# Sorted rows that carry their expert shares, and one VectorE reduction per gathered tile

## What is computed

```python
x = L0_attn_x                      # (8, 512, 256)
xn = _layernorm(x)
scores = sigmoid(xn @ gate_w)      # (tokens, 32)
topk_w, topk_i = top_k(scores, 6)
topk_w = topk_w / (sum(topk_w) + 1e-20)
combine = sum(one_hot(topk_i, 32) * topk_w[..., None], axis=1)
act = silu(xn @ wg[e]) * (xn @ wu[e])
routed = einsum('tef,efd,te->td', act, wd, combine)
x = x + attention(xn) + routed + shared(xn)
```

## Time and profile before

| | |
|---|---|
| median of 3 runs | 1434.82 us (1430.83 to 1435.81) |
| the profiled execution | 1436.87 us, its span 1434.7 us |
| PE busy | 1302.8 us (91%) |
| DVE busy | 938.8 us (65%) |
| ACT busy | 851.0 us (59%) |
| POOL busy | 588.7 us (41%) |
| mean granted PE clock | 0.977 of 2.4 GHz |

### The profile page before, as it was taken

One profiled execution on the slowest core, in us unless ns is written; L12 is line 12 of the kernel. 1 busy time (PEld: TensorE's weight loads), 2 busy tenths in 40 slices (PEclk: granted clock), 3 DMA queues, 4 the chain that ended last, 5 costly groups with the idle time before them and its releaser, 6 DMA issues. The chain is left out here.

```text
span 1434.7 us, 24478 instructions
## 1 busy us (share of the span) xinstructions
PE 1302.8 (91%) x7385; PEld 963.7 (67%) x7385; DVE 938.8 (65%) x3727; ACT 851.0 (59%) x2294; POOL 588.7 (41%) x607
## 2 busy tenths in 40 slices
PE   4899769999999999889999999988899898998996
PEld 3566446777776777677888888865566666666664
DVE  3578678777777777423664333327888888888784
ACT  1455437677666667445566666646666666666663
POOL 1111127776676777400000000014666666566663
PEclk8899979999999999999999999989999999999998
DMA  9776652323228222298855555532233332332321
GB/s 345 309 266 249 247 201 96 111 82 107 100 82 301 103 96 78 70 286 310 268 179 177 177 176 179 177 121 70 85 101 85 103 107 78 107 107 78 107 74 56
DMA packets 133844, 216.98 MB, mean 151 GB/s; under 512 B 14743, under 2 KB 108631, under 8 KB 128855
## 3 DMA queue, kind: packets, MB, share of 16 engines
q1 hardware_dynamic: 101462, 152.48, 31.2%
q0 software_dynamic: 18432, 50.36, 10.8%
q10 hardware_dynamic: 13824, 12.59, 2.8%
HBM read 103.70 MB, written 111.67 MB: 150 GB/s over the span
## 5 line engine op out<-in xcount | busy, mean ns | idle before, releaser
L1708 ACT ACTIVATE l_prob<-l_prob,l_negmax 128x512 f32<-128x512 f32 (+3 forms) x256 | 142.1, 556 | 154.3 <-DVE l_negmax L1794 154.2
L1063 POOL DMA_INDIRECT sorted_x<-f_xn_row,slot_no x192 | 204.5, 1065 | 49.9 <-issue 49.3
L1219 ACT ACTIVATE f_prob<-f_prob,f_negmax 128x512 f32<-128x512 f32 (+3 forms) x256 | 142.6, 558 | 122.0 <-DVE f_negmax L1292 120.0
L1601 PE MATMUL ps<-l_kt,l_qt 128*128 128x512 f32 (+3 forms) x512 | 176.9, 452 | 39.1 <-DVE l_qt L1772 22.4
L1539 POOL DMA_INDIRECT l_rows<-sorted_y,slot_no x192 | 185.6, 967 | 49.1 <-issue 41.6
L2126 DVE TENSOR_TENSOR act_f<-hidden,ps 128x96 f32<-128x96 f32 x224 | 56.9, 254 | 211.1 <-ACT hidden L2101 210.3
L2063 PE MATMUL ps<-wgu_sb,xt_e 128*128 x896 | 185.0, 329 | 7.5 <-ACT xt_e L2096 7.5
L1122 PE MATMUL ps<-kt_s,f_qt 128*128 128x512 f32 (+3 forms) x512 | 170.4, 447 | 5.7 <-DVE f_qt L1283 4.4
L1292 DVE CUSTOM_DVE_ANT_0 f_prob<-ps,mask_add 128x512 f32<-128x512 f32 (+3 forms) x256 | 121.0, 486 | 81.0 <-issue 80.1
L1794 DVE CUSTOM_DVE_ANT_0 l_prob<-ps,mask_add 128x512 f32<-128x512 f32 (+3 forms) x256 | 122.0, 485 | 71.8 <-issue 70.6
L2063 PEld LDWEIGHTS ps<-wgu_sb,xt_e 128*128 128x128 f32 x896 | 141.0, 191 | 10.1 <-issue 9.9
(11 more groups left out here) (202 smaller groups left out, 2940.1 us busy)
## 6 DMA issues: line engine op xcount, KB each, us to landing
sorted_x<-zeros SPq DMA_DIRECT2D x14, 2048.0 KB, 8.9
rows_in<-sorted_x SPq DMA_DIRECT2D x112, 256.0 KB, 3.0
sorted_y<-rows_out SPq DMA_DIRECT2D x112, 256.0 KB, 2.1
wgu_sb<-in_wgu SPq DMA_DIRECT2D x16, 384.0 KB, 5.3
x_in<-in_x SPq DMA_DIRECT2D x8, 512.0 KB, 9.7
xn_dram<-xn SPq DMA_DIRECT2D x8, 512.0 KB, 3.7
base_dram<-x_in SPq DMA_DIRECT2D x8, 512.0 KB, 2.9
nqt_dram<-nqt_out SPq DMA_DIRECT2D x8, 512.0 KB, 3.9
```

The lines of the kernel that those rows point to most:

```text
L1063: pool.indirect_dma_start(sorted_x, bass.IndirectOffsetOnAxis(ap=slot_no[:, t, k:k + 1], axis=0), xn_row[buf][:], None).then_inc(scattered ...
L1219: act.activation(prob[:, i, qt, 0:w], prob[:, i, qt, 0:w], ACT.Exp, bias=negmax[:, i, qt:qt + 1], scale=-1.0, accum_out=rowsum[:, g // 2 % ...
L1601: mm = pe.matmul(s_ps[k % 2][:, 0:w], qt[g // 2 % 2][g % 2][:, n * P:w], kt[b - HB][:, 0:w], start=True, stop=True)
L1708: act.activation(prob[:, i, qt, 0:w], prob[:, i, qt, 0:w], ACT.Exp, bias=negmax[:, i, qt:qt + 1], scale=-1.0, accum_out=rowsum[:, g // 2 % ...
```

## The change

`sorted_x` rows become 288 wide (HW): 256 columns of the normalised token and the token's 32 entries of `comb`, its share for each expert, zero where it has none. In the first heads POOL copies `comb` of the tile into the right part of `xn_row` before the six indirect DMAs, with a wait on its own semaphore between. The fills of zeros and the loads of rows grow from 256 to 288 columns. In the experts the product on DVE is a `SCALAR_TENSOR_TENSOR` that also multiplies by the share, which stands in column `H + expert` of the row; DVE reads the expert list for that into its own register, once for four tiles. The load of new rows waits for `act_done` in place of `xt_ready`. `find_shares` goes. In the last heads the base of a tile is loaded into a seventh row of `rows`, and one `TENSOR_REDUCE` adds the seven rows, read as `p h k`: its innermost index walks over the seven rows, 1024 bytes apart. It stands at the end of the odd head, behind the fourth maximum.

```diff
-ZCOLS = 2048
+HW = H + NE
+ZCOLS = 2304
@@ first heads, POOL
                     pool.wait_ge(row_loaded[buf], 16 * (t // ROWS) + 16)
+                    pool.tensor_tensor(xn_row[buf][:, H:HW], comb[:, t, :], one[:].to_broadcast([P, NE]), ALU.mult)\
+                        .then_inc(shares_put, 1)
+                    pool.wait_ge(shares_put, t + 1)
@@ experts, SP
-                    sp.wait_ge(xt_ready, 2 * r + (2 - 2 * AHEAD))
+                    sp.wait_ge(act_done, 2 * r + (2 - 2 * AHEAD))
@@ experts, DVE
+                        share = rows_in[(j - 1) // 2 % AHEAD][:, 1 - par, bass.ds(H + expert_of(j - 1), 1)]
                         dve.wait_ge(silu_done, c + 1)
-                        dve.tensor_tensor(act_f[1 - par][:], hidden[1 - par][:], gu_ps[1 - par][:, FE:2 * FE],
-                                          ALU.mult).then_inc(act_done, 1)
+                        dve.scalar_tensor_tensor(act_f[1 - par][:], hidden[1 - par][:], share,
+                                                 gu_ps[1 - par][:, FE:2 * FE], ALU.mult, ALU.mult).then_inc(act_done, 1)
-                    if i in (1, 2) and par == 0:
-                        last.find_shares(dve, PAIRS * (i - 1) + j // 2, comb, slot_of, slot_top)
@@ last heads, DVE
-                dve.scalar_tensor_tensor(total[par][:], rows[par][:, k, :], share[:, c, k:k + 1],
-                                         (base if k == 0 else total)[par][:], ALU.mult, ALU.add).then_inc(totalled, 1)
+            def sum_tile(bt, g):
+                c = bt.gathered_tile(g, PACE + 1)
+                if c is None:
+                    return
+                par, n = c % NROW, c // NROW
+                dve.wait_ge(gathered[par], 16 * TOPK * n + 16 * TOPK)
+                dve.wait_ge(rows_base[par], 16 * n + 16)
+                if c > 0:
+                    dve.wait_ge(base_kept, 16 * c)
+                dve.tensor_reduce(total[par][:], rows[par][:].rearrange("p k h -> p h k"), AX.X, ALU.add)\
+                   .then_inc(totalled, 1)
@@ last heads, DVE, end of step
                 if now:
                     maxima(bt.now, g, 3)
+                if par == 1:
+                    sum_tile(bt, g)
```

More of the change, by code:

```diff
@@ L855, in __init__ @@
         self.wd = whole.sb("wd_sb", [FE, NE, H])
[L856 removed]
+        self.rows_in = [ctx.enter_context(nc.sbuf_tensor(f"rows_in{i}", [P, 2, HW], F32)) for i in range(self.AHEAD)]
         self.expert_row = ctx.enter_context(nc.sbuf_tensor("expert_row", [1, 2 * P], U8))
@@ L921, in heads_first @@
     carry = sb("f_carry", [P, 2 * TT])
-    xn_row = [room_c.sb(f"f_xn_row{i}", [P, H]) for i in range(ROWS)]
+    xn_row = [sb(f"f_xn_row{i}", [P, HW]) for i in range(ROWS)]
     carrier = sb("f_carrier", [P, ROWS])
-    qa = sb("f_qa", [P, S])
+    qa = room_c.sb("f_qa", [P, S])
     qb = sb("f_qb", [P, S])
@@ L1388, in heads_last @@
     carry = sb("l_carry", [P, 2 * TT])
-    wq_s, wvo_s, rope_t, kt, nqt, nkv, share = last.wq, last.wvo, last.rope, last.kt, last.nqt, last.nkv, last.share
-    base = [sb(f"l_base{i}", [P, H]) for i in range(NROW)]
+    wq_s, wvo_s, rope_t, kt, nqt, nkv = last.wq, last.wvo, last.rope, last.kt, last.nqt, last.nkv
     total = [sb(f"l_total{i}", [P, H]) for i in range(NROW)]
-    rows = [sb(f"l_rows{i}", [P, TOPK, H]) for i in range(NROW)]
+    rows = [sb(f"l_rows{i}", [P, TOPK + 1, H]) for i in range(NROW)]
     carrier = sb("l_carrier", [P, NROW])
@@ L1863, in step @@
                     between(bt, g)
-                if par == 1:
-                    sum_rows(bt, g, 0)
                 if now:
                     maxima(bt.now, g, 1)
-                if par == 0 and not bt.piece(g):
-                    sum_rows(bt, g, 5)
-                if par == 1:
-                    sum_rows(bt, g, 1)
-                    if nxt:
-                        queries_rope(*nxt)
-                    sum_rows(bt, g, 2)
+                if par == 1 and nxt:
+                    queries_rope(*nxt)
                 if now:
@@ L2118, in _, with read_experts, expert_of @@
                 dve.memset(primer[:, par:par + 1], 0.0).then_inc(out_stored[par], 16)
+            dve.wait_ge(expert_loaded, 16)
             def steps(i, js):
+                read = {}
+                def read_experts(j):
+                    first = ITER // 4 * i + j // 4
+                    read[j // 4] = dve.value_load(words[0:1, bass.ds(first, 1)], min_val=0, max_val=ALL_LAST)
+                def expert_of(j):
+                    if j // 4 not in read:
+                        read_experts(j)
+                    return (read[j // 4] >> 8 * (j % 4)) & (NE - 1)
                 for j in js:
```

56 lines of the change are left out of this document (16 added, 40 removed).

## The result

The changed kernel takes 1465.51 us (median of 4 runs, 1462.86 to 1467.68); the kernel before, run beside it, 1432.82. The ratio is 1.0215, with a 95% interval of 1.0183 to 1.0247: slower, where the forecast said 1402 us and at most 1458. The profiled execution spans 1465.0 us against 1434.7 before.

A forecast was written before the change was run, and what follows sets the result against it. DVE's summing of gathered rows was taken to hold the last heads above PE's pace. 1436.9 - 32.3 - 6.4 + 1.0 + 1.5 + 2.7 + 0.8 = 1404.2, less 2.05 to the median: 1402 us, range 1389 to 1458.

The forecast's parts named there:

- Where the time stood: Last heads: pairs take 13.72 and 14.38 us against PE's 11.03 and 13.67, 49.6 us lost to DVE's summing of rows.
- The reduction's duration: Last heads: one reduction of 1792 elements takes 2.02 us, replacing 4.08 us of sums on DVE per tile.
- both bounds: Last heads, reduction time: 2.02 us at the contiguous rate, 3.89 us if each element takes twice the time.
- The halved rate: Rival, last heads: the stride makes the reduction 3.89 us, adding 52.4 us, so 1455 us in all; chance 0.32.
- the partial penalty: Rival, last heads: the stride makes the reduction 2.95 us, so 1428 us in all; chance 0.07.
- break-even point: Last heads: from about 3.2 us of reduction on, 28 x 1.2 us has eaten the gain of 33.
- The walk against PE: Last heads, DVE's order against PE's: stalls of 0.54 and 0.22 us, pairs of 11.57 and 13.89, gaining 32.3 and 6.4 us.
- POOL as a limit: Rival, last heads: POOL's DMA issues do not fit, short pairs near 12.5 us, 14 us lost, 1416; chance 0.05.
- The experts: Experts stage: moved load wait, crowded start and longer rows cost 1.5 us; longer product and register load 0.
- The register work: Experts, DVE: list load plus 0.2 us of register work hides in 0.96 us idle; cost 0, at most 17 us.
- The start: Start: larger zero fills cost 2.7 us before the first `xn_dram` store and 0.8 at POOL's first scatter.
- The rest of the kernel: After the last pair of the last heads: a change of 0 us.

The follow-up runs named there:

- e6: Changed kernel with the seven-row reduction replaced by one sum of two rows, 256 elements (five rows left out): 1402.0 us, ratio 0.9775.
- e1: Changed kernel with the reduction walking its 1792 elements contiguously, so not summing the right rows: 1421.95 us, ratio 0.9909.
- e12: Changed kernel with the seven elements of each sum 1 to 256 elements apart, eight distances in turn by tile, sums not right: 1458.1 us, ratio 1.015.
- e5: Changed kernel with the experts' DVE product plain again, without share or register work; longer rows and moved wait stay: 1457.87 us, ratio 1.0159.
- e3: Kernel before, with only SP's load of rows waiting for `act_done` in place of `xt_ready`: 1438.96 us, ratio 1.0017.
- e14: Changed kernel with the plain two-operand product in the experts, while DVE still reads the expert numbers: 1455.29 us, ratio 1.015.
- e7: Changed kernel with 1056 instead of 1024 bytes between the rows of a tile that the reduction adds: 1475.67 us, ratio 1.028.
- e8: Changed kernel with three contiguous sums in three places for the reduction, and SP's store issued ahead of its load: 1410.57 us, ratio 0.9818.
- e13: Changed kernel with the experts' product always taking the share of expert 0, so no expert number is read on DVE: 1457.02 us, ratio 1.0162.

## Why the prediction was wrong

**Where the time stood** was right. PE's pace, read from the first heads, came out to 0.02 us in e6 (11.02 to 11.05 and 13.69, against 11.03 and 13.67).

**The reduction's duration** is the step that failed. The sum took 2.02 us from two contiguous reductions. For such elements the figure is exact (2.015 in e1), but these lie 1024 bytes apart, and it took 3.32. The stage is 37.7 us longer for it than in e1. The text saw both bounds and a rule of the Trainium skill (SBUF — State Buffer, section on the two sides of the memory) that spoke against the change, and put the reduction at the lower bound, since the contiguous rows already move only one element at a time. e12 refutes that reason: the rate still falls by 1.64. The halved rate had a third of the chance, and the partial penalty of 2.95 us only 0.07; the truth lay between the two. Its break-even point of about 3.2 us nearly held for this stage: 3.32 us gave 6.5 us more than before, where the same sum has 3.4 (28 x 1.30 - 33).

**The walk against PE** gave 11.57 and 13.89 us for a reduction of 2.02. e1 has 11.86 to 12.00 and 14.01 to 14.13, and more with a merge: 397.1 us in the stage, where the forecast has 390.6. DVE's chain was right: from the start of the last maximum of the odd head at 1095.23 to PE's next block at 1100.17 it is 4.94 us, by the walk 4.95. In the short pairs of 11.86 us the stall is 0.52 us (5.37 us from the start of one block of 128 columns to that of the next, for 4.85 in e6), by the walk 0.54. The walk left out two things. PE's block behind that one waits for the third maximum, which DVE does right behind the second (the maximum ends at 1100.47, and the wait at 1100.51): the six matmuls take 2.19 us instead of 1.89, 0.3 more in each short pair. And in the short pairs of 12.00 POOL's subtraction holds a query sum, for 0.97 us instead of 0.73, so that the last maximum starts 0.15 us later (e1, POOL, then DVE):

```profile
1093.37 1.28 POOL L1548 TENSOR_TENSOR l_lat_lo<-l_lat,l_lat_hi 128x512 fp32r<-128x512 f32 x1 [0.82 <-ACT l_lat_hi L1728]
...
1094.23 0.97 DVE L1775 TENSOR_TENSOR l_qt<-l_qa,l_qb 64x512 f32<-64x512 f32 x1
```

That each further us of reduction lengthens every pair by as much held from 2.02 us on: 1.30 us more gave 37.7 us in the stage.

**POOL** as a limit was rightly charged nothing: the subtraction of the earlier trace rows, mean 1.63 us before, takes 1.28 after, and from 1019 to 1380 us PE's wait for it is 1.3 us in all. The mean pair there is 14.02 us, not 13.82 (15 of 13.72 and 13 of 14.37), which changes nothing. That POOL would now meet the query sum of DVE was not seen.

**The experts** are the second failed step. Of SP's new wait the text said that the store behind it waited longer anyway. That looked at when the store is let go, not at what stands ahead of it in the queue: the order load, store with no time between them makes the store land in 3.5 us for 2.1, and two buffers just cover that, with 0.37 us to spare (e5). By one execution 5.6 us came by the wait alone (e3), and 1.5 was allowed for everything. The register work was costed as the load of the list, ahead of the wait; that part was hidden, as said (e14). The arithmetic on the number stands behind the wait and delays every product by 0.26 us, and the store with it; it was put inside DVE's idle time at 0.2 us. The order of instructions under "The change" has it behind `silu_done` already. The stage lost 17.9 us, where 1.5 stood in the sum.

**The start** was right in kind: DVE's second layer norm was due at 51.6 and came at 51.0, and both waits of the earlier trace rows grew, by 2.5 and 1.2 us. That the stage grew by 2.7 us to the digit is in part luck: in the 17 executions after the one of before it ends anywhere from 196.8 to 200.2 us, and at 196.8 in e3, whose fills are the old ones.

```profile
51.02 1.38 DVE L657 TENSOR_SCALAR xn<-x_in,mv,rstd 128x256 f32<-128x256 f32 x4 [13.89 <-DMA xn_dram<-xn]
...
208.70 0.24 POOL L1062 TENSOR_TENSOR f_xn_row<-comb,f_one 128x32 f32<-128x32 f32 x1 [13.34 <-DMA sorted_x<-zeros]
```

**The rest of the kernel**, put at nothing, took 2.1 us more. It holds the last reductions: with contiguous elements it took 38.9 us (e1), with one short sum 42.3 (e6), with three sums 41.7 to 42.5, and 44.5 to 47.8 in all others that have a strided reduction.

**What stays open**: the cost in the experts is known only to a few us, since each kernel has one profiled execution, and what begins each long delay there was not traced.

## What to carry to other kernels

Before folding several operations into one, write down the distance in bytes between the elements that the new operation reads one after the other, and price it from rows with that distance; where there are none, do not let the better bound stand as the likely one. One long block on the engine that paces PE can lose what several short ones gain, even with less work in all. Where a wait on a DMA queue is moved, look at which transfer now goes out directly ahead of which, at what a later signal does to everything behind it in that queue, and at how much time the buffers leave to spare, since several small delays add up there without a loss until nothing is left; and look in the order of instructions at which one takes a wait, since everything of that engine behind it is uncovered.

## What the runs showed of the hardware

- A reduction of 1792 fp32 elements on DVE takes 2.02 us with neighbours 4 or 8 bytes apart and 3.28 to 3.48 us at 16 to 1024 bytes (3.49 at 1056; e12, e7): a step between 8 and 16 bytes.
- Sums of two operands, both in the core's memory and contiguous, ran at 0.954 us for 768 elements, 0.690 for 512 and 0.398 for 256, and were not held by POOL in the places where e8 has them (one of 96 was, for 1.71 us), though the 256-element additions of before averaged 0.72 us.
- A store of 256 KB lands in 2.1 us when it is issued ahead of a load of 256 or 288 KB on the same queue, and in 3.3 to 3.6 us when it is issued 0.4 us behind one (medians).
- A DVE product whose operand has an address from a register begins 0.29 us after the end of the operation that it waits for (median of the 224 tiles), and 0.03 us after it with a fixed address (e13).
- A DVE sum of two operands in the core's memory still meets POOL: in e1 the query sum of 64x512 takes 0.97 us where it starts during POOL's subtraction, 1.65 us where it starts just after the subtraction has begun, and 0.69 to 0.73 where it starts near its end or without it.
